# The integral image of a four-image layer chain: planes normalised on ScalarE, two rows per transpose, triangular products over eight rows

## The reference

```python
def _gn(v, G=16, eps=1e-5):
    ...
    return ((g - m) / jnp.sqrt(s + eps)).reshape(v.shape)
...
integ = jnp.cumsum(jnp.cumsum(x, axis=-1), axis=-2)
...
A = _grid_sample_border_bilinear(integ, off_tl)
...
return (A + D - Bt - Ct) / area
```

## Time and profile before

| | us |
|---|---|
| median of 3 runs | 23,072.08 |
| lowest, highest run | 23,068.33, 23,091.53 |
| the profiled execution: its span | 23,062.7 |
| the four integral stages in it (first memset to last addition) | 392.1, 380.6, 380.7, 396.1 |

### The profile page before, as it was taken

One profiled execution on the slowest core, in us unless ns is written; L12 is line 12 of the kernel. 1 busy time (PEld: TensorE's weight loads), 2 busy tenths in 40 slices (PEclk: granted clock), 3 DMA queues, 4 the chain that ended last, 5 costly groups with the idle time before them and its releaser, 6 DMA issues. The chain is left out here.

```text
span 23062.7 us, 439024 instructions
## 1 busy us (share of the span) xinstructions
PE 21104.9 (92%) x142360; PEld 13332.1 (58%) x142360; DVE 15532.4 (67%) x23763; ACT 7714.9 (33%) x21928; POOL 10668.1 (46%) x8568
## 2 busy tenths in 40 slices
PE   6998998989989989899899898998998978888889
PEld 4664446567744465666544555774445545565556
DVE  4445665666679966566799756667997566666644
ACT  3663331146632211455322114663221112222222
POOL 0000000068866620677666306886663067777710
PEclk9999998999999989999999889999998889899999
DMA  3331001645533326455333255553332566666643
GB/s 88 69 69 33 31 31 60 135 109 119 118 86 98 97 83 134 106 114 112 88 97 98 83 131 111 118 118 87 96 98 79 131 128 137 135 142 135 140 89 78
DMA packets 884628, 2312.45 MB, mean 100 GB/s; under 512 B 259300, under 2 KB 511464, under 8 KB 765132
## 3 DMA queue, kind: packets, MB, share of 16 engines
q1 hardware_dynamic: 463312, 1363.96, 26.7%
q0 software_dynamic: 419840, 928.94, 15.9%
HBM read 1914.87 MB, written 385.13 MB: 100 GB/s over the span
## 5 line engine op out<-in xcount | busy, mean ns | idle before, releaser
L1768 POOL DMA_INDIRECT e_got<-table,e_idx x6144 | 7788.5, 1268 | 2880.2 <-issue 1651.8
L1784 POOL DMA_INDIRECT e_got<-table,e_idx x2048 | 2590.8, 1265 | 865.9 <-issue 591.9
L1158 DVE SCALAR_TENSOR_TENSOR b_acc<-b_z,b_dwc,b_acc 112x1024 f32<-112x1024 f32 x2112 | 2610.8, 1275 | 4.2
L517 PE MATMUL a_p_qk<-a_wst,a_stack 125*128 125x192 f32 x12288 | 2453.4, 336 | 25.5 <-DMA a_stack<-in_xp 7.6
L971 PE MATMUL b_p_conv<-b_z,b_diag_a 64*64 64x512 f32 x19008 | 2279.3, 600 | 4.4 <-DVE b_g_a L1172 4.4
L517 PEld LDWEIGHTS a_p_qk<-a_wst,a_stack 125*128 125x128 f32 x12288 | 2017.0, 191 | 423.9 <-issue 330.2
L953 PEld LDWEIGHTS b_p_z<-const,b_ym 128*66 128x66 f32 (+2 forms) x12672 | 1511.8, 172 | 1102.8 <-issue 889.1
L1822 DVE TENSOR_TENSOR e_got<-e_got,e_wt 128x1536 f32<-128x1536 f32 x1024 | 1765.4, 1748 | 204.1 <-DMA e_got<-table,e_idx 192.8
L953 PE MATMUL b_p_z<-const,b_ym 128*66 128x128 f32 (+2 forms) x12672 | 1857.4, 285 | 15.4 <-ACT b_z L1070 15.4
L1056 ACT ACTIVATE b_xp<-b_p_in 128x128 f32<-128x128 f32 x1056 | 293.2, 278 | 4689.9 <-PE b_p_in L932 4677.3
L1276 POOL DMA_DIRECT2D i_x<-planes x128 | 66.5, 520 | 3522.5 <-issue 2192.3
(11 more groups left out here) (293 smaller groups left out, 39684.4 us busy)
## 6 DMA issues: line engine op xcount, KB each, us to landing
e_got<-table,e_idx POOLq DMA_INDIRECT x8192
b_x<-planes SPq DMA_DIRECT2D x264, 395.1 KB
a_stack<-in_xp SPq DMA_DIRECT2D x256, 387.0 KB
c_stack<-planes SPq DMA_DIRECT2D x256, 387.0 KB
d_stack<-planes SPq DMA_DIRECT2D x256, 387.0 KB
table<-i_acc SPq DMA_DIRECT2D x256, 384.0 KB, 2.3
b_xr<-planes SPq DMA_DIRECT2D x264, 197.5 KB
planes<-b_out SPq DMA_DIRECT2D x264, 197.5 KB
```

The costliest lines, as they stand in the source:

```text
L517: m = pe.matmul(dst_, st[:, row, dx + 128 * t:dx + 128 * t + 128], wst[:, dx, 0:2 * C2], start=(dx == 0), stop=False)
L1158: dve.scalar_tensor_tensor(out=a, in0=rows, scalar=dwc[0:M[D], D, k:k + 1], in1=a, op0=ALU.mult, op1=ALU.add).then_inc(chain, 1)
L1768: pool.indirect_dma_start(out=self.got[q][:, t, c * REC:(c + 1) * REC], out_offset=None, in_=self.flat, in_offset=bass.IndirectOffsetOnAxi ...
L1784: pool.indirect_dma_start(out=self.got[q][:, t, c * REC:(c + 1) * REC], out_offset=None, in_=self.flat, in_offset=bass.IndirectOffsetOnAxi ...
```

## The change

1. **Scale and shift move to ScalarE.** The matrix `norm`, its folding and its product are gone. VectorE copies scale and shift into two columns, and ScalarE normalises a strip in one activation, 113 partitions x 1024, from `x` to a new pair of buffers `xn`, two strips ahead of the products. The load of a strip waits for this activation instead of the tokens.
2. **Two rows by one transpose.** A strip is loaded as two halves of four rows, one on partitions 0 to 48, one on 64 to 112 (two DMAs instead of one). `pe.transpose` turns 113 partitions x 128 pixels at once: 8 transposes a strip instead of 16 f32 matmuls. ScalarE and VectorE pick 48 of every 64 columns (`tokens_of`).
3. **The wait of the tokens** asks for one half less: `t_lower >= n * 2 - 1 + h`.
4. **Products for eight rows at once**: `p_p[h]` is two banks (512 columns for `prefix`, 512 for `prefix1`), 14 products of 384 columns instead of 28 of 192.
5. **No carry copy.** `acc` has eight rows; the first addition of a strip reads the last row of the other buffer. An addition takes 48 columns from each of the two banks. In the first strip a copy takes its place.

```diff
+def tokens_of(bank):
+    return bank[:].rearrange("p (y q c) -> p q y c", q=2, c=64)[:, :, :, 1:CP]
...
-        x = [sb(f"x{i}", [WIDE, SROWS, WP]) for i in range(2)]
-        fold, norm = sb("fold", [CP, 128]), sb("norm", [WIDE, CP])
+        x = [sb(f"x{i}", [PAIR, HROWS, WP]) for i in range(2)]
+        xn = [sb(f"xn{i}", [PAIR, HROWS, W]) for i in range(2)]
+        scale, shift = sb("scale", [PAIR, 1]), sb("shift", [PAIR, 1])
...
-        p_p = [pb(f"p_p{i}") for i in range(4)]
-        p_n = pb("p_n")
+        p_p = [pb(f"p_p{h}", (128, 1024)) for h in range(2)]
...
-                        pool.wait_ge(t_ready, (b * S + u * 2 + k + 1) * 2)
+                        pool.wait_ge(normed, b * S + u * 2 + k + 1)
                         pool.sem_inc(turn, 1)
-                        pool.dma_start(x[k][0:CP], planes(src, b, 0, CP, (u * 2 + k) * SROWS + 1, SROWS)).then_inc(loaded[k], 16)
+                        for q in range(2):
+                            pool.dma_start(x[k][64 * q:64 * q + CP], planes(src, b, 0, CP, (u * 2 + k) * SROWS + HROWS * q + 1, HROWS)).then_inc(loaded[k], 16)
...
-                    pe.wait_ge(loaded[par], load * 16)
+                    pe.wait_ge(normed, n + 1)
                     for h in range(2):
-                        pe.wait_ge(t_lower, n * 2 + h)
-                        for r in range(SROWS):
-                            mm = pe.matmul(p_t[h][:, r * C:(r + 1) * C], x[par][:, r, 1 + 128 * h:129 + 128 * h], norm[:, 1:CP], start=True, stop=True)
+                        pe.wait_ge(t_lower, n * 2 - 1 + h)
+                        for y in range(HROWS):
+                            mm = pe.transpose(p_t[h][:, 128 * y:128 * y + PAIR], xn[par][:, y, 128 * h:128 * h + 128], env.c("ident")[0:PAIR, 0:PAIR])
...
-                    for i in range(4):
-                        a, h = divmod(i, 2)
-                        pe.wait_ge(summed, n * 4 + i - 3)
+                    for h in range(2):
+                        pe.wait_ge(summed, n * 2 - 1 + h)
                         for s, mat in enumerate(("prefix", "prefix1")):
-                            o = p_p[i][:, 0:4 * R2].rearrange("p (y s c) -> p y s c", s=2, c=C)[:, :, s, :]
+                            o = p_p[h][:, 512 * s:512 * s + SROWS * C]
...
+                def normalise(n, par, load):
+                    act.wait_ge(loaded[par], load * 32)
+                    act.wait_ge(t_ready, (n - 1) * 2)
+                    act.activation(xn[par][:], x[par][:, :, 1:1 + W], ACT.Identity, bias=shift[:], scale=scale[:]).then_inc(normed, 1)
...
                     if more:
                         halves(n + 1, 1 - par)
+                    if more2:
+                        normalise(n + 2, par, load + 1)
...
-                        dve.wait_ge(summed, n * 4)
-                        dve.tensor_copy(acc[par][:, :, 0, :], acc[1 - par][:, :, SROWS, :]).then_inc(carried, 1)
...
-                            ins = dve.tensor_tensor(acc[par][:, h, 4 * a + r + 1, :], acc[par][:, h, 4 * a + r, :], p_p[i][:, r * R2:(r + 1) * R2], ALU.add)
+                                above = (acc[par][:, h, r - 1, :] if r else acc[1 - par][:, h, SROWS - 1, :]).rearrange("p (s c) -> p s c", s=2)
+                                ins = dve.tensor_tensor(to, above, part, ALU.add)
```

More of the change, by code:

```diff
@@ L1292, in tokens, with step @@
                         mm.then_inc(t_ready, 1)
[L1294 to L1301, removed]
+                def step(n, par, load, first, more, more2):
                     if more:
-                        tokens(n + 1, 1 - par, load if par == 0 else load + 1)
+                        tokens(n + 1, 1 - par)
@@ L1304, in step @@
                     pe.wait_ge(t_lower, n * 2 + 2)
-                    for i in range(4):
-                        a, h = divmod(i, 2)
-                        pe.wait_ge(summed, n * 4 + i - 3)
-                        half = [[tok[par][j][:, k, a * 4 * C:(a + 1) * 4 * C].rearrange("p (y c) -> p y c", c=C) for j in range(2)] for k in range(2)]
+                    half = [[tok[par][j][:, k, :] for j in range(2)] for k in range(2)]
+                    for h in range(2):
+                        pe.wait_ge(summed, n * 2 - 1 + h)
@@ L1320, in step @@
                         mm.then_inc(p_ready, 1)
-                pipeline(pe, begin, step)
+                pipeline(pe, lambda: tokens(n0, 0), step)
             @block.scalar
@@ L1329, in halves, with begin, step @@
                         act.wait_ge(t_ready, n * 2 + h + 1)
-                        act.wait_ge(p_ready, (n - 1) * 4)
-                        upper(act, tok[par][0][:, h, :], p_t[h][:, 0:SROWS * C], t_copied)
-                def step(n, par, load, first, more):
+                        act.wait_ge(p_ready, (n - 1) * 2)
+                        upper(act, tok[par][0][:, h, :].rearrange("p (q y c) -> p q y c", q=2, c=C), tokens_of(p_t[h]), t_copied)
+                def begin():
+                    normalise(n0, 0, l0 + 1)
+                    normalise(n0 + 1, 1, l0 + 1)
+                    halves(n0, 0)
+                def step(n, par, load, first, more, more2):
                     if more:
                         halves(n + 1, 1 - par)
-                pipeline(act, lambda n0, load: halves(n0, 0), step)
+                    if more2:
+                        normalise(n + 2, par, load + 1)
+                pipeline(act, begin, step)
             @block.vector
             def _(dve):
-                for sem, k in ((summed, 4), (carried, 1), (chain, 4 * 3), (t_lower, 2)):
+                for sem, k in ((summed, 2), (chain, LINKS), (t_lower, 2)):
                     start(dve, sem, k)
@@ L1344, in _ @@
                     dve.tensor_copy(t[:], env.c(m)).then_inc(mats_ready, 1)
-                for t in (*x, norm):
+                for t in (*x, scale, shift):
                     dve.memset(t[:], 0.0).then_inc(mats_ready, 1)
-                dve.wait_ge(mats_ready, 7 * (b + 1))
+                dve.wait_ge(mats_ready, 8 * (b + 1))
                 def halves(n, par):
@@ L1351, in halves, with begin, step @@
                         dve.wait_ge(t_copied, n * 2 + h + 1)
-                        dve.wait_ge(p_ready, (n - 1) * 4)
-                        lower(dve, tok[par][1][:, h, :], p_t[h][:, 0:SROWS * C], tok[par][0][:, h, :], t_lower)
-                def begin(n0, load):
-                    dve.wait_ge(p_ready, n0 * 4)
-                    make_fold(dve, env, "c", b, fold[:], 128, fold_ready, b * 2)
-                    dve.wait_ge(turned, b + 1)
-                    dve.tensor_copy(norm[0:CP, :], p_n[0:CP, 0:CP]).then_inc(norm_ready, 1)
+                        dve.wait_ge(p_ready, (n - 1) * 2)
+                        lower(dve, tok[par][1][:, h, :].rearrange("p (q y c) -> p q y c", q=2, c=C), tokens_of(p_t[h]),
+                              tok[par][0][:, h, :].rearrange("p (q y c) -> p q y c", q=2, c=C), t_lower)
+                def begin():
+                    r, nmr = env.norm["c"]
+                    for q in range(2):
+                        dve.tensor_copy(scale[64 * q:64 * q + CP, :], r[:, b:b + 1]).then_inc(norm_ready, 1)
+                        dve.tensor_copy(shift[64 * q:64 * q + CP, :], nmr[:, b:b + 1]).then_inc(norm_ready, 1)
                     halves(n0, 0)
-                def step(n, par, load, first, more):
+                def step(n, par, load, first, more, more2):
                     if more:
```

76 lines of the change are left out of this document (42 added, 34 removed).

## The result

| | median us | ratio to before, interval |
|---|---|---|
| before, 4 runs | 23,074.18 | |
| after, 4 runs (22,264.61 to 22,273.67) | 22,268.25 | 0.9651 [0.9638, 0.9665] |

The change is faster by 3.5%. The profiled execution after the change took 22,273.67 us with a span of 22,272.1 us. The span fell by 23,062.7 - 22,272.1 = 790.6 us.

A forecast was written before the change was run, and what follows sets the result against it. TensorE was taken to set the pace of the integral stage. A stage of 16 + 32 x 6.0 = 208 us instead of 387.4, four times, saves 718 us: 23,062.7 - 718 + 9.4 = 22,354 us; range 22,260 to 22,630.

The forecast's parts named there:

- the period of 6.0 us: Integral stage, time per eight-row strip: the slower engine's, 5.68 to 6.34 us, taken in the middle as 6.0.
- VectorE's strip: VectorE's work per strip in the integral stage: sixteen additions 4.56 us, two subtractions 0.558 each; 5.68 us, 5.17 to 6.3.
- The old products at full clock: TensorE's 28 products of 192 columns per strip before the change: 0.1125 us each at full clock, 3.15 together.
- TensorE's strip at half clock: TensorE's work per strip after the change: eight transposes 1.71 us plus fourteen products 4.63, 6.34 us at half clock.
- The start of a stage: From the integral stage's first memset to its first addition: about 16 us, 14 to 18, where it was 30.2.
- The normalisation: ScalarE's one 113x1024 activation per strip: 1.06 us, hidden because it runs two strips ahead.
- The load's turn: Issue, landing and normalising of a strip's load: 7.1 us, up to 9.1, hidden within 12.0 us for two strips.
- Rival A: Clock stays at half all through the integral stage: period 6.34 us, stage 220 us, time 22,402 us; chance 0.22.
- Rival B: Each transpose on TensorE is two records: 5.68 to 8.05 us a strip, 22,470 us, or 22,626 always at half clock; chance 0.17.
- Rival C: TensorE waits out each chain of VectorE's additions: period 10.7 us, stage 358 us, time 22,955 us; chance 0.06.
- Rival D: Slower: the strip's load becomes the bound; at 24 us landing, period 13.2 us, stage 438 us, time 23,276 us; chance 0.03.
- One of the marks: Sign in the after profile: TensorE's waits for the additions above 1 us a strip would prove the forecast's overlap wrong.

## Why the prediction was right, and where it was off

Stage time saved against the 1549.5 us of before, from the sums above:

| | us saved |
|---|---|
| wait alone | 211 |
| products and chains alone | 73 |
| both of these | 488 |
| all but the wait | 490 |
| tokens and wait, products of 192 columns | 815 |
| the whole change | 790 |

**The forecast's mechanism held.** It said that the whole change stands in the integral stage, that the wait of the tokens goes, and that VectorE becomes the bound wherever TensorE is at full clock. All three stand in the rows, and the third was tried from both sides: more records on TensorE did not lengthen the stages (plain matmuls, narrow products), and a shorter VectorE shortened them (joined additions).

**What a part is worth depends on the others.** The wait is worth 211 us alone, 1476.9 - 1061.4 = 416 beside the wide products and 300 beside all the rest. The wide products are worth 73 us alone, 1338.6 - 1061.4 = 277 once the wait is relaxed, and minus 25 beside the new tokens, where VectorE sets the pace. So no part has a share of the 790 us that could be named by itself.

**The step that was off is the period of 6.0 us,** "the middle" of 5.68 and 6.34, "as the clock has been at either level in this stage". Measured it is (189.8 - 15.7) / 32 = 5.44. Both halves of the step were wrong. TensorE is at half clock only in about a fifth of the stage (0.88 to 0.92 is a mix of 0.5 and 1.0), so that VectorE's strip nearly always sets the period, and its end of the range was the nearer one. No row of the kernel before gave that share for the new one, so the middle was a guess. And this strip was mis-sized, 5.33 instead of 5.68: two subtractions take 0.94 from start to start of what follows, not 2 x 0.558, and sixteen additions 4.39, not 4.56. The end of one instruction overlaps the start of the next, and a busy time from a group can't be added up as if it did not. Against that, some strips lose 0.37 at their end. The four stages came out 4 x (208 - 189.8) = 73 us shorter than forecast; the remaining 13 of the 86 us are the 9.4 that were added for the way from the span to the median, where the median after the change lies 3.8 us below the profiled span.

**The other terms.** The old products at full clock were priced by the tokens' record, 0.1125; the run with the wait alone shows 0.11 for them, so nothing hangs on it. TensorE's strip at half clock was 6.04, not 6.34: the products 4.63 as forecast from three quarters of the 512-column ones, the transposes 1.41 instead of 1.71. At full clock fourteen products at 0.175 make 2.45 instead of 2.87. The start of a stage took 15.7 of the 16 us. The normalisation was priced at 1.06 from the copy and took 1.24; it is hidden, as said: ScalarE waits for a load only at the start of the stage (10.4 us, L1334). The Trainium skill ("ScalarE: Activation LUTs", What ACT_TABLE_LOAD costs) states that each operand that is a column of one number per partition, as scale and bias are here, adds some 93 ns to an activation; by it the two would add an estimated 0.19 us, and the trace agrees, 1.24 being 0.17 above the copy of about as many columns. The load's turn is 1.1 + 3.5 + 1.24 = 5.8 us of the 10.9 that two strips take; 7.1 of 12 was the forecast. The DMA share is 0.60, forecast 0.56.

**Rival A, half clock all through, is refuted** by windows at 0.88 to 0.92. With plain matmuls instead of the transposes it is 0.96. The Trainium skill ("TensorE: Matmul & The Clock Gate", Part 4) says that the full clock does not come on in transpose mode; its reason, that this "doesn't count as PE-busy the same way", is weaker than what the prediction made of it. The trace does not agree: the full clock stayed on over a strip with eight transposes in the change (1.00 from 3846.0 to 3851.5) and over 29 such strips with narrow products (1.00 from 3780.0 to 3938.7). Why the change itself falls back to half clock now and then is open. **Rival B, two records per transpose,** is refuted by 256 records for 256 transposes; the plain matmuls in their place do show two. **Rival C, the engines in turn,** did not come, but it lay closer than its chance of 0.06 says: with the old wait back, the strip takes 7.7 us, partly in turns. The fit that was worked out against it rests on the relaxed wait. **Rival D, the load,** had no part: loads land in 3.5 us.

**One of the marks was badly set.** Waits of TensorE for the additions "that add up to more than 1 us a strip" were to prove the overlap wrong. They add up to 43.6 / 32 = 1.36, and the overlap is right: they are what the engine that is not the bound does with its spare time. The mark should have been the idle time of VectorE: 15.5 and 15.2 us in the first stage before the additions and the subtractions. Of these 8.7 are at the start, and some 13 are the gaps inside the chains, 4.45 - 16 x 0.253 = 0.40 a strip; about 9 us are left. Its busy time was put at 180 us, the strip's whole length; the profile counts 158.5, without the gaps between additions.

**What stays open.** The normalisation on ScalarE and the turning of two rows at once were not taken apart. What part of the 488 us is the clock's is not settled, nor why it rose, nor where the last 18 of the 211 us of the wait come from. How late the load and ScalarE could be made before they count was not tried.

## What to carry to other kernels

Find the strip time of every engine before adding up what a change takes off one of them: once the next engine sets the pace, further savings are worth nothing (here the products of 384 columns beside the new tokens), and the next edit to make is on that engine (here one addition for two halves, 112 us of stage time). Do not price a part by a run with that part alone: the same one-line wait was worth 211, 416 and 300 us here, the same products 73, 277 and minus 25. Where a period lies between the values of two clocks, say how much of the time each clock holds; if no row tells, the middle is a guess and should be called one.

## What the runs showed of the hardware

- A TensorE that hardly ever stands still can be at half clock most of the time. With the wait alone removed it was 96% busy at a clock of 0.65, and in the strip shown the clock fell during 32 records of f32 matmuls with 48 columns each; with the wide products and transposes, 69% busy, it was 0.88 to 0.92.
- Transposes do not keep the full clock off: with narrow products it was 1.00 over 29 strips with eight transposes each.
- A transpose of 113 x 128 f32 is one record, the plain f32 matmul that does the same two. Eight transposes take 1.41 us at half clock and 0.70 at full (3849.60 to 3850.30 in the run with joined halves); the 16 records of the plain matmuls take 1.71 at full (3777.43 to 3779.14).
- An addition of 128x192 with one operand in PSUM takes 353 ns, of 128x96 253 ns; that the products lie in two banks instead of one adds nothing (253 against 252 ns).
- An fp32r product of 384 columns costs 0.175 us at full and 0.320 at half clock (3773.58 to 3776.78 for ten); one of 192 columns 0.11 (3869.70 to 3869.92 for two, with the wait alone removed) and 0.217. Twice the columns cost about 1.5 times as much.
